# Four graph networks on one core: the last four steps of each pass of networks 2 and 3 written out behind the loop

## What is computed

```python
h = jnp.maximum(_layernorm(x, axis=-1), 0.0)
x = x + _L2_gnn_ref(h, edge_index, ...)      # network 2: four layers (passes over all edges), 8 heads
...
x = x + _L3_gnn_ref(h, edge_index, edge_attr_18, ...)   # network 3: one pass, 4 heads, 18 attributes an edge
# one layer of network 2
alpha = jnp.sum(q * k, axis=-1) / float(np.sqrt(D_HEAD))
amax = jax.ops.segment_max(alpha, dst, num_segments=n)
ex = jnp.exp(alpha - amax[dst])
denom = jax.ops.segment_sum(ex, dst, num_segments=n)
out = jax.ops.segment_sum(((ex / denom[dst])[:, :, None] * v).reshape(-1, f), dst, num_segments=n)
```

## Time and profile before

| | before |
|---|---|
| runs | 12692.91, 12690.47, 12689.09 us |
| median | 12690.47 us |
| profiled execution: span | 12691.5 us |
| mean granted TensorE clock | 0.693 |
| PE busy | 7569.9 us (60%) |
| DVE busy | 7905.7 us (62%) |
| ACT busy | 6283.5 us (50%) |
| POOL busy | 8886.0 us (70%) |

### The profile page before, as it was taken

One profiled execution on the slowest core, in us unless ns is written; L12 is line 12 of the kernel. 1 busy time (PEld: TensorE's weight loads), 2 busy tenths in 40 slices (PEclk: granted clock), 3 DMA queues, 4 the chain that ended last, 5 costly groups with the idle time before them and its releaser, 6 DMA issues. The chain is left out here.

```text
span 12691.5 us, 185977 instructions
## 1 busy us (share of the span) xinstructions
PE 7569.9 (60%) x46394; PEld 5754.5 (45%) x46395; DVE 7905.7 (62%) x21707; ACT 6283.5 (50%) x14083; POOL 8886.0 (70%) x9142
## 2 busy tenths in 40 slices
PE   6766455555551112333566676667666766667998
PEld 5666322222220002333366636663666456645766
DVE  8888666656653224333477767776777677775555
ACT  8333333333323332666466646664666456635666
POOL 0777677767767774777677767776777677765775
PEclk9666677767765555555777787778777877775555
DMA  0000111121121113222544544444444444432223
GB/s 33 2 2 2 32 39 39 39 37 39 39 36 40 40 39 42 54 54 53 107 132 132 128 106 132 132 131 102 133 131 132 97 136 132 131 79 57 71 71 63
DMA packets 820871, 949.30 MB, mean 75 GB/s; under 512 B 481435, under 2 KB 557648, under 8 KB 820444
## 3 DMA queue, kind: packets, MB, share of 16 engines
q0 software_dynamic: 343040, 637.31, 21.9%
q1 hardware_dynamic: 477532, 309.04, 9.1%
HBM read 859.26 MB, written 86.39 MB: 75 GB/s over the span
## 5 line engine op out<-in xcount | busy, mean ns | idle before, releaser
L806 POOL DMA_INDIRECT work<-t,idx x3328 | 3174.5, 954 | 1125.0 <-issue 1014.1
L1654 POOL DMA_INDIRECT work<-t,idx x3328 | 3184.5, 957 | 1058.7 <-issue 1013.5
L818 ACT ACTIVATE work<-iota,loc 128x128 f32<-128x128 f32 (+1 forms) x6672 | 2034.6, 387 | 3251.5 <-DVEq L1112 1920.6
L1115 DVE TENSOR_TENSOR work<-work,ps 128x192 f32 x2496 | 883.6, 354 | 1230.3 <-PE ps L1139 929.7
L1139 PE MATMUL ps<-work 128*128 128x192 bf16 x2496 | 418.5, 308 | 1732.1 <-SPq L813 1657.6
L1749 PE MATMUL ps<-work 128*128 x6784 | 1346.7, 382 | 137.4 <-ACT work L831 73.1
L1749 PEld LDWEIGHTS ps<-work 128*128 128x128 f32 x6784 | 1322.9, 298 | 179.5 <-issue 166.2
L600 POOL DMA_INDIRECT tab<-work x784 | 863.3, 1101 | 562.3 <-DVE work L453 315.4
L1761 PE MATMUL ps<-work 128*128 128x136 f32 x6656 | 1248.2, 344 | 10.1 <-DVE work L1815 9.6
L728 POOL DMA_INDIRECT tab<-work x784 | 808.6, 1031 | 529.1 <-POOLq L39 283.3
L1139 PEld LDWEIGHTS ps<-work 128*128 128x128 bf16 x2496 | 235.2, 114 | 2048.0 <-issue 1078.1
(11 more groups left out here) (426 smaller groups left out, 17015.1 us busy)
## 6 DMA issues: line engine op xcount, KB each, us to landing
work<-t,idx POOLq DMA_INDIRECT x7488
node<-pl SPq DMA_DIRECT2D x424, 256.0 KB, 3.4
work<-pl SPq DMA_DIRECT2D x54, 512.0 KB
work<-pl SPq DMA_DIRECT2D x106, 256.0 KB, 3.3
tab<-work POOLq DMA_INDIRECT x1568, 2.1
t<-work SPq DMA_DIRECT2D x196, 128.0 KB, 1.8
x<-work SPq DMA_DIRECT2D x196, 64.0 KB, 1.8
h<-work SPq DMA_DIRECT2D x28, 448.0 KB, 2.6
```

The costliest lines, as they stand in the source:

```text
L806: pool.indirect_dma_start(X[:, j % 4, n, :], None, table, bass.IndirectOffsetOnAxis(ap=idx[k][:, 8 * j + n:8 * j + n + 1], axis=0)).then_i ...
L818: t = act.activation(P[:, b, n, :], iota[:, :], ACT.Square, scale=-1.0, bias=loc[k][:, bass.ds(a + n, 1)])
L1115: added.on(dve.tensor_tensor(av, av, part(z, n), ALU.add))
L1654: pool.indirect_dma_start(X[:, j % 4, n, M - KD:W], None, table, bass.IndirectOffsetOnAxis(ap=idx[k][:, NT * j + n:NT * j + n + 1], axis=0 ...
```

## The change

In networks 2 and 3 the hardware loops of PE, DVE and ACT run `Q // 4 - 1` = 11 iterations in place of 12. The last four steps stand written out behind them, and in those:

- network 2: the last step issues no `queries` (PE), no `onehot_nodes` (ACT), and its two halves of `scores` are replaced by `adds`, the four adds that stood between them (DVE);
- network 3: the last step has no `turned`, `views` and `scores`; the last two have no splits, squares and one-hots for steps 52 and 53;
- SP no longer loads node numbers and attributes for steps 52 and 53, nor signals them, and the end waits for them are gone.

POOL's instructions and everything in the other 51 steps stay. The diff, cut to its core (network 3's PE and ACT change in the same way as those shown):

```diff
@@ network 2, SP
                     for j in range(Q):
                         for z in range(2):
-                            land_unit(sp, j + 1, z)
-                            sp.wait_ge(lbfree.sem, lbfree.up())
                             if j + 1 < Q:
+                                land_unit(sp, j + 1, z)
+                            if j + 1 < Q:
+                                sp.wait_ge(lbfree.sem, lbfree.up())
+                            if j + 2 < Q:
                                 load_places(sp, LB, lb, places_, 2 * (j + 2) + z)
@@ network 2, ACT
-                def act_step(act, a, w, first):
+                def act_step(act, a, w, first, last=False):
...
-                    onehot_nodes(act, own, PT, LB, lb, lbfree, 0, ptd)
+                    if not last:
+                        onehot_nodes(act, own, PT, LB, lb, lbfree, 0, ptd)
@@ network 2, PE
-                    queries(pe, a + NT, 0)
+                    if not last:
+                        queries(pe, a + NT, 0)
...
-                    pe.wait_ge(usedp.sem, usedp.up())
-                    queries(pe, a + NT, 1)
+                    if not last:
+                        pe.wait_ge(usedp.sem, usedp.up())
+                        queries(pe, a + NT, 1)
...
-                    with pe.Fori(1, Q // 4) as i:
+                    with pe.Fori(1, Q // 4 - 1) as i:
                         for w in range(4):
                             pe_step(pe, i * (4 * NT) + NT * w, w, False)
                         for s in waited:
                             s.back(pe)
+                    for w in range(4):
+                        pe_step(pe, NT * (Q - 4 + w), w, False, w == 3)
+                    for s in waited:
+                        s.back(pe)
@@ network 2, DVE
+                def adds(dve, u, i):
+                    av = places(dve, u, i)
+                    dve.wait_ge(parts.sem, parts.up())
+                    for n in range(4 * i, 4 * i + 4):
+                        add(dve, av, n)
...
-                    scores(dve, (w + 1) % 4, 1 - u, 0, 1, has1)
+                    if final:
+                        adds(dve, 1 - u, 1)
+                    else:
+                        scores(dve, (w + 1) % 4, 1 - u, 0, 1, has1)
...
-                    scores(dve, (w + 1) % 4, 1 - u, 1, 2, has1)
+                    if final:
+                        adds(dve, 1 - u, 2)
+                    else:
+                        scores(dve, (w + 1) % 4, 1 - u, 1, 2, has1)
...
-                    with dve.Fori(1, Q // 4) as i:
+                    with dve.Fori(1, Q // 4 - 1) as i:
                         for w in range(4):
                             dve_step(dve, i * (4 * NT) + NT * w, w, False)
                         dve.wait_ge(v.sem, v.c)
                         for s in waited:
                             s.back(dve)
+                    for w in range(4):
+                        dve_step(dve, NT * (Q - 4 + w), w, False, w == 3)
+                    dve.wait_ge(v.sem, v.c)
+                    for s in waited:
+                        s.back(dve)
@@ network 3, DVE
-                    split_rest(dve, u)
+                    if ahead == 2:
+                        split_rest(dve, u)
...
-                    scores(dve, (w + 1) % 4, 1 - u, 0, 1, has1)
+                    if ahead:
+                        scores(dve, (w + 1) % 4, 1 - u, 0, 1, has1)
+                    else:
+                        adds(dve, 1 - u, 1)
+                        dve.sem_inc(flfree.sem, 1)
...
-                    split_low(dve, u)
+                    if ahead == 2:
+                        split_low(dve, u)
```

More of the change, by code:

```diff
@@ L1762, in weigh_, with pe_step @@
                     t.then_inc(parts.sem, 1)
-                def pe_step(pe, a, w, first):
+                def pe_step(pe, a, w, first, last=False):
                     u, b1 = w % 2, (w + 3) % 4
@@ L2776, in _ @@
                             s.back(act)
+                    for w in range(4):
+                        act_step(act, NT * (Q - 4 + w), w, False, min(3 - w, 2))
+                    for s in waited:
+                        s.back(act)
                     act.wait_ge(pfree.sem, pfree.up(2))
@@ L2817, in weigh_, with pe_step @@
                     t.then_inc(parts.sem, 1)
-                def pe_step(pe, a, w, first):
+                def pe_step(pe, a, w, first, last=False):
                     u, b1 = w % 2, (w + 3) % 4
                     has1 = not (first and w == 0)
-                    turned(pe, 1 - u, 0)
+                    if not last:
+                        turned(pe, 1 - u, 0)
                     pe.wait_ge(evd.sem, evd.up())
@@ L2831, in pe_step @@
                         weigh_(pe, b1, 1 - u, 1)
-                    views(pe, a + NT, 1 - u, 0)
+                    if not last:
+                        views(pe, a + NT, 1 - u, 0)
                     pe.wait_ge(rowd.sem, rowd.up())
@@ L2837, in pe_step @@
                         weigh_(pe, b1, 1 - u, 2)
-                    turned(pe, 1 - u, 1)
+                    if not last:
+                        turned(pe, 1 - u, 1)
                     pe.wait_ge(md.sem, md.up())
@@ L2842, in pe_step @@
                         weigh_(pe, b1, 1 - u, 3)
-                    pe.wait_ge(used.sem, used.up())
-                    views(pe, a + NT, 1 - u, 1)
+                    if not last:
+                        pe.wait_ge(used.sem, used.up())
+                        views(pe, a + NT, 1 - u, 1)
                 @block.tensor
@@ L2937, in scores, with dve_step @@
                             t.then_inc(flfree.sem, 1)
-                def dve_step(dve, a, w, first):
+                def dve_step(dve, a, w, first, ahead=2):
                     u, b1 = w % 2, (w + 3) % 4
@@ L3059, in _ @@
                             s.back(dve)
+                    for w in range(4):
+                        dve_step(dve, NT * (Q - 4 + w), w, False, min(3 - w, 2))
+                    dve.wait_ge(v.sem, v.c)
+                    for s in waited:
+                        s.back(dve)
                     dve.wait_ge(ex.sem, ex.up())
```

65 lines of the change are left out of this document (36 added, 29 removed).

## The result

| | before | after |
|---|---|---|
| median of 12 runs | 12690.76 us | 12714.35 us |
| lowest, highest | 12688.35, 12695.79 | 12705.76, 12723.31 |
| profiled execution: span | 12691.5 us | 12705.2 us |

The changed kernel takes 1.0018 times as long, 95% interval 1.0009 to 1.0026: 11 to 33 us more. 12698 was forecast, with "within 0.2%" as the likeliest outcome; the time lies 16 us higher and inside the range, just at the edge of 0.2%. One thing has to be kept in mind for all that follows: the profiled execution of the changed kernel (12707.0 us as a run) is one of its fastest, 7 us under its median.

What follows compares the result with a forecast made beforehand. No engine was full; each pass was a chain through DVE and PE, DVE setting its end. Passes 0 and 1 -13.8, pass 2 +17.4, pass 3 +16.8, network 3 -12.7: +7.7 on 12690.5 gives 12698 us, range 12648 to 12720.

Steps and rivals of the forecast that it cites:

- The mechanism: DVE's loops in passes 2 and 3 touch a fourth block of 128 instructions and refetch at each jump back; chance 0.62.
- The rival of pages of 256 instructions: DVE keeps two pages of 256: only pass 3 refetches, network 3 no longer; sum -46, 12644 us; chance 0.10.
- The tails alone count: Rival: neither pass 2 nor pass 3 refetches; sum -39.7, 12651 us; chance 0.08.
- The tails: Ends of network 2's passes: dropped last-step work saves 6.3 us a pass, 6.9 with flags in passes 0, 1 and 3.
- the flags' wait of step 51: DVE's wait for flags ahead of step 51 goes: 0.6 us in each of passes 0, 1 and 3.
- Network 3: forecast -12.7: Network 3: -9.7 us at its end from dropped work, -3.0 from one loop-back that becomes a fall-through.
- The price of a jump: DVE's 10 loop-backs in each of passes 2 and 3 cost 3.0 us more each, +30 us a pass.
- The "dear jump" rival: Passes 2 and 3: each loop-back costs 5 to 5.5 us, two fetches in turn; 12739 to 12749 us; chance 0.07.
- Absorbed: Near the ends of passes 2 and 3, DVE gains on POOL, so 6.3 us of the delay vanishes in each.
- the wait of step 50: DVE's 6.74 us wait for flags at step 50 of passes 2 and 3: 6.3 of it goes in each.
- The range's lower half: Down to 12648 us: neither pass refetches (12651, chance 0.08) or one of passes 2 and 3 alone (12675, chance 0.13).

Runs made afterwards that it cites:

- e1: The changed kernel with 50 more DVE instructions (satisfied waits) at the start of pass 2, moving the later loops: 12628.52 us, ratio 0.9951 to the kernel before.
- e4: The changed kernel run again with no edit, for a second profile: 12722.35 us.
- e3: The kernel before with only network 3's part of the change: 12681.44 us, ratio 0.999 to the kernel before.
- e2: The kernel before with only satisfied DVE waits added at the starts of the stages, moving all five loops: 12738.25 us, ratio 1.0035.
- e5: Loops of 11 iterations, four full steps written out, nothing dropped, 60 waits at pass 2's start: 18067.35 us, ratio 0.9983 to the kernel before.
- e7: The kernel before with 60 waits (30 DVE instructions) at the start of pass 3: 18093.15 us, ratio 0.9991 to the kernel before.
- e9: The same kernel as e7, run again: 18464.36 us, ratio 0.9992 to the kernel before.
- e10: The same kernel as e5, run again: 18452.08 us, ratio 0.9979 to the kernel before.
- e11: The same kernel as e5, run once more: 18470.38 us, ratio 0.9986 to the kernel before.

## Why the prediction was right, and which terms were off

- **The mechanism** held in each point of the refetch: passes 2 and 3 refetch, pass 1 (359) does not, network 3 keeps its price. The rival of pages of 256 instructions said that only pass 3 would refetch and network 3 would be freed; pass 2's 5.16 us a jump and network 3's unchanged 84.9 us exclude it, and the unit of the page "Runtime: NRT & Kernel Launch" of the Trainium skill (section "Instruction fetch mechanics") with it, on this chip: what is kept goes by blocks of 128 instructions, and a loop may touch three of them. Its warning that a taken branch can force a fetch is what decided this change. "The tails alone count" is excluded by the same rows.
- **The tails.** Forecast -6.9, -6.9, -6.3, -6.9, together -27. The rows of the last step came to a few tenths (3.21 for 3.2), but between the first jumps e1 shows only -3.1, -7.9, -6.3 and -3.6, together -21. Where I let the flags' wait of step 51 go it did go: 0.60 us in pass 0 has no row after. What took the rest is the flags' wait one step earlier, at step 50. Passes 0 and 3, first before, then e1:

```profile
7287.05 0.42 DVE L1871 TENSOR_TENSOR_SCAN work<-tri,ps 128x128 f32<-128x128 bf16 x1 [4.30 <-DMA work<-sf]
...
11198.74 0.42 DVE L1871 TENSOR_TENSOR_SCAN work<-tri,ps 128x128 f32<-128x128 bf16 x1 [5.75 <-DMA work<-sf]
...
7286.87 0.42 DVE L1889 TENSOR_TENSOR_SCAN work<-tri,ps 128x128 f32<-128x128 bf16 x1 [9.36 <-DMA work<-sf]
...
11177.89 0.42 DVE L1889 TENSOR_TENSOR_SCAN work<-tri,ps 128x128 f32<-128x128 bf16 x1 [9.13 <-DMA work<-sf]
```

  5.1 and 3.4 us more. Less these waits the four stages of e1 are 7.0 to 8.2 us shorter, 1 to 4 of them in the ten iterations ahead. So three of the tails gave about what was forecast (6.2 to 6.7 us), and pass 3's 3.3. The wait scatters from one execution to the next, 3.9 us in the changed kernel's pass 0 and 7.9 in e4's, and my sum held it fixed. Network 3: forecast -12.7, measured -12.7 (-11.4 in e3).
- **The price of a jump** is the term that failed: "3.0 us more in each of 10 loop-backs". I took network 3's price less that of leaving its loop, where the neighbour to take was network 2's own jump of 1.6. Measured are 5.16 - 1.6 = 3.6 in pass 2 and 4.43 - 1.6 = 2.8 in pass 3, and in network 3 itself 2.7. Per iteration it is 3.8 and 3.7 (84.6 and 84.4 against e1's 80.8 and 80.7), so 37 us a pass and not 30: +14 to the sum. In pass 3 a second wait shows what the rest is. Here is an iteration's start there, timeline of DVE, 10599:

```profile
10599.30 0.69 DVE L1827 TENSOR_TENSOR work<-work,ps 128x512 f32<-128x512 f32 x1 [4.17 <-issue]
...
10602.01 0.29 DVE L1836 TENSOR_TENSOR work<-work,ps 128x136 f32 x1 [0.93 <-DVE work L1836]
```

  An add that otherwise waits 0.15 us for the add ahead waits 0.93. It stands some 11 instructions behind the jump, where the block ends by my count. The same waits in e4, pass 2 and then pass 3:

```profile
DVE work L1836 <- DVE work L1836: 12.3, 80, 0.2
...
DVE work L1836 <- DVE work L1836: 18.1, 80, 0.9
```

  Pass 2, 40 instructions from its block's end, has nothing of it; pass 3 has 0.6 us an iteration. The "dear jump" rival had this mechanism; it costs 0.6 to 0.8 us, not a second fetch of 4. A few tenths an iteration are left that I can't name.
- **Absorbed.** Forecast 6.3 us in each of passes 2 and 3. Against e1 the changed kernel's stages are 28.2 and 28.9 us longer, its ten iterations 37.7 and 36.9: 9.5 and 8.0 were absorbed, part of it because e1 has those long flags' waits. In pass 3 the wait of step 50, which I had forecast to go, went in part: from 5.75 us to 3.06 (0.69 in e4). In pass 2, 6.74 us, it is 0.36 after:

```profile
9904.58 0.42 DVE L1889 TENSOR_TENSOR_SCAN work<-tri,ps 128x128 f32<-128x128 bf16 x1 [0.36 <-DMA work<-sf]
```

- **The sum again** with terms measured against e1: tails -21 - 12.7, jumps 20 x 3.73 = +74.6, absorbed -17.5: +23.4. The error of 16 us is then the jump's price (+14.6) and the tails (+6), less what more was absorbed (-5). That the medians lie 23.6 apart, so near, is luck: the terms come from one execution each, and the profile of the changed kernel against that of the kernel before gives +19.2 for the same stages. There the forecast's +7.7 was missed by 4.5 us in pass 2 and 8.5 in pass 3, and by 1.5 the other way in passes 0 and 1 together.
- **The range's lower half** held cases with fewer refetches. The upper end was closer to what happened: each of my bounds for the jump (0 to 3.65 more) came from network 3, and pass 2 with 3.8 an iteration lies outside them. A bound by the nearest row needs the row of the same loop for what is taken away.

## What to carry to other kernels

Writing steps out behind a loop costs nothing where they stand, but it moves every later loop. Here a loop of 303 or 338 DVE instructions is free of refetch only while its end lies within 384 of the edge of the block of 128 in which it begins, and a few dozen idle instructions ahead of a loop, where the engine waits anyway, are worth 27 to 37 us a loop. Where it doesn't wait they cost 0.10 us each. So after each change of length compare the instruction queue's packets in a loop, and when a kernel gets slower with less work, look there before looking at the work.

## What the runs showed of the hardware

- The jump back of a DVE loop costs 1.3 to 1.6 us when its target is still there, and 4.1 to 5.3 when not, with 5 to 6 packets of 8 KB an iteration; 5.2 and 5.3 at places 88 and 86, 4.1 at 103, 4.4 at 117 with 0.6 to 0.8 more at the next block. The packets are the same at every place that refetches: 57 or 58 in ten iterations, 7 or 8 where nothing is refetched.
- The edge is sharp: 385 instructions by my count stay, 389 don't.
- An instruction of satisfied semaphore waits takes DVE 0.10 us (62 of them 6.2 us in e2).
- Two executions of one kernel differed by 5.3 us in the ten iterations of one pass while its jumps differed by 1.1, and by 4.0 us in one wait for flags. The runs of the changed kernel spread over 17.6 us, those of before over 7.4 in the same comparison and 14.2 in e1's.
- The same kernels took 18000 us and more in some of the comparisons, with DVE waiting 4 to 9 us at a time in mid-step, on nothing that the records name, and satisfied waits taking 0.7 or 1.4 us at times. There e5, e7, e9, e10 and e11 lay within 0.3% of the kernel before.
